# Message pass of a two-layer graph network: block sums added up in PSUM banks, one-hot matrices built on two engines, first LayerNorm inside the pass

## The reference

```python
# 6250 nodes, 256 features; 100000 edges (src, dst, edge_weight)
# layer 0: msg = (x[dst] @ node_w + node_b) * W(edge_weight)      W: radial basis and a small MLP
agg = segment_sum(msg, src)
h = x + agg
out = (h - mean(h)) / sqrt(var(h) + 1e-5) * ln_g + ln_b
x1 = layernorm(x + out * sigmoid(out @ gate_w + gate_b))
# layer 1: weighted means of x1's halves over the edges, both directions, added to x1, then a LayerNorm
```

## Time and profile before

| | us |
|---|---|
| median of 3 runs (lowest, highest) | 5071.47 (5069.38, 5073.18) |
| the profiled execution: its time | 5067.16 |
| its span, first to last instruction | 5065.1 |
| busy TensorE, VectorE, ScalarE, GpSimd | 3600.8, 2815.1, 2019.5, 3207.5 |

### The profile page before, as it was taken

How to read it: one execution, slowest core, us unless ns; L and a number is a source line. 1 busy time by engine, 2 the same in 40 slices (tenths; PEclk the granted TensorE clock), 3 DMA queues, 4 the chain that set the end, 5 groups by cost and what they waited for, 6 DMA issues and landing times.

```text
span 5065.1 us, 77985 instructions
## 1 busy us (share of the span) xinstructions
PE 3600.8 (71%) x16432; PEld 2653.5 (52%) x16433; DVE 2815.1 (56%) x7139; ACT 2019.5 (40%) x5492; POOL 3207.5 (63%) x3263
## 2 busy tenths in 40 slices
PE   6999999999999999788875544444443556565662
PEld 4655555555555555466653344444443555555552
DVE  4665656556566565466668522222222666666667
ACT  1555455554555545488884211111111222222221
POOL 0777777777777777600003477777777777777772
PEclk8999999999999999999997655555555776777775
DMA  7544444444444444476661111111111433334334
GB/s 191 134 136 135 135 138 136 137 135 135 137 135 136 135 135 138 137 226 216 215 212 40 32 53 53 53 53 53 53 53 59 113 102 102 102 105 107 102 102 77
DMA packets 464444, 588.32 MB, mean 116 GB/s; under 512 B 70163, under 2 KB 385171, under 8 KB 464406
## 3 DMA queue, kind: packets, MB, share of 16 engines
q0 software_dynamic: 128512, 317.64, 20.5%
q1 hardware_dynamic: 335894, 270.26, 18.9%
HBM read 391.39 MB, written 196.22 MB: 116 GB/s over the span
## 4 chain that ended last, share of the span: by engine, by line
POOL 41%; issue 23%; PE 12%; DVE 11%; DVEq 5%; DMA 4%; ACT 2%; POOLq 1%; SPq 0%; ACTq 0%
POOL s_rows L495 14%; POOL d_rows L528 14%; POOL arena L487 12%; DVE arena L1369 5%; DMA arena<-s_rows 3%; DVEq L313 3%; PE ps L908 3%; PE ps L989 3%; PE ps L980 2%; DVE agg L1234 1%; PE ps L933 1%; DVEq L1369 1%; DVE arena L1318 1%; ACT arena L643 1%; POOLq L287 1%
## 5 line engine op out<-in xcount | busy, mean ns | idle before, releaser
L528 POOL DMA_INDIRECT d_rows<-arena,adr x832 | 809.7, 973 | 302.8 <-issue 253.1
L487 POOL DMA_INDIRECT arena<-y_rows,idx x784 | 754.5, 962 | 354.2 <-issue 238.6
L541 POOL DMA_INDIRECT arena<-x_half,idx x832 | 808.2, 971 | 253.5 <-issue 250.2
L495 POOL DMA_INDIRECT s_rows<-arena,adr x784 | 770.4, 983 | 245.7 <-issue 244.8
L869 PE MATMUL ps<-f3s,arena 128*128 128x256 f32 x3136 | 728.2, 386 | 129.1 <-ACT arena L587 129.0
L958 PE MATMUL ps<-agg,arena 128*128 x1664 | 430.0, 440 | 521.7 <-ACT arena L699 521.6
L858 PE MATMUL ps<-arena,f2s 128*128 128x512 f32 x1568 | 706.1, 593 | 0.0
L869 PEld LDWEIGHTS ps<-f3s,arena 128*128 128x128 f32 x3136 | 581.1, 190 | 233.8 <-issue 120.9
L958 PEld LDWEIGHTS ps<-agg,arena 128*128 128x128 f32 x1664 | 370.0, 328 | 575.6 <-issue 575.6
L1369 DVE TENSOR_TENSOR arena<-arena,ps 128x129 f32 x1664 | 481.0, 289 | 333.0 <-issue 87.4
L989 PE MATMUL ps<-arena 128*128 128x129 f32 x1664 | 338.2, 367 | 425.4 <-issue 261.9
(11 more groups left out here) (195 smaller groups left out, 5850.9 us busy)
## 6 DMA issues: line engine op xcount, KB each, us to landing
arena<-s_rows SPq DMA_DIRECT2D x52, 2088.0 KB, 8.4
arena<-d_rows SPq DMA_DIRECT2D x52, 1040.0 KB
arena<-wrow SPq DMA_DIRECT2D x392, 64.0 KB
arena<-env_row SPq DMA_DIRECT2D x392, 64.0 KB
d_rows<-arena,adr POOLq DMA_INDIRECT x832, 2.3
arena<-x_half,idx POOLq DMA_INDIRECT x832, 2.5
s_rows<-tpl_s SPq DMA_DIRECT2D x98, 130.5 KB, 7.0
arena<-y_rows,idx POOLq DMA_INDIRECT x784
```

The lines of the kernel that those rows point to most:

```text
L487: pool.indirect_dma_start(gath[b][:, t, :], None, y_rows, bass.IndirectOffsetOnAxis(ap=idx[b][:, t:t + 1], axis=0)).then_inc(gathered[b], 16)
L495: pool.indirect_dma_start(s_rows, bass.IndirectOffsetOnAxis(ap=adr[b][:, t:t + 1], axis=0), msg[b][:, t, :], None).then_inc(scattered[b], 16)
L528: pool.indirect_dma_start(d_rows, bass.IndirectOffsetOnAxis(ap=adr[b][:, t:t + 1], axis=0), drow[b][:, t, :], None).then_inc(scattered_d[b ...
L541: pool.indirect_dma_start(gath2[b][:, t, :], None, x1_half, bass.IndirectOffsetOnAxis(ap=idx[b][:, t:t + 1], axis=0)).then_inc(gathered2[b ...
```

## The change

- In the pass every tile's product is accumulated by TensorE itself into one of four PSUM banks (SLOTS), the block's number modulo 4, at an offset that TensorE reads into a register from a new table slot_of; it reads the block number of the group's last tile too, and waits on a semaphore against it until that bank is free. VectorE no longer adds per tile: per block it waits for the block's last tile, adds the bank to x (`take_out`), and clears the bank.
- One-hots: ScalarE builds two tiles of four as before (BY_ACT = 2), GpSimd the other two with one is_equal each. The one-hot buffers are four instead of two, the message buffers four of 8 tiles (PT) instead of two of 16.
- x is loaded into agg during the message stage, block by block; the clearing of agg goes.
- The first LayerNorm is done by VectorE inside the pass, after each 7 blocks, with ln_g and ln_b (two operations of 128x1792). The roots come from a bit shift and three Newton steps on VectorE, twelve operations on 128x7.
- In the node stage that is left, transposes of chunk c + 1 are ahead of chunk c's gate products, with two buffers for each.
- Before the message stage: slot_of takes five operations on one partition, block ends two more, and each of two earlier computations loses two.

```diff
--- before.py
+++ after.py
...
+        s_buf = [take(PT, RW) for _ in range(4)]
+        hot = [take(GT, P) for _ in range(4)]
+        apart = [take(GT, P) for _ in range(2)]
         node_at = at
-        x_c = [take(CB * H) for _ in range(3)]
-        h_c = [take(CB * H) for _ in range(3)]
+        resid = take(NB * H)
+        h_c = [resid[:, c * CB * H:(c + 1) * CB * H] for c in range(CHUNKS)]
         at = 0
-        tr_c, gate_c, res_c = take(CB * H), take(CB * H), take(CB * H)
+        tr_c, gate_c = [take(CB * H) for _ in range(2)], [take(CB * H) for _ in range(2)]
...
+
+            for b in range(2):
+                sp.wait_ge(y_out[b], 16 * slot_uses(CHUNKS, b))
+            sp.wait_ge(table_mm, 2)
+            sp.dma_start(agg_n[:, 0:2, :], x_n[:, 0:2, :]).then_inc(x_in, 16)
             with sp.Fori(2, G0 // 4) as i:
                 for b in range(4):
                     load_de(4 * i + b, i, b)
                 blank_rest(i)
+                sp.dma_start(agg_n[:, bass.ds(i, 1), :], x_n[:, bass.ds(i, 1), :]).then_inc(x_in, 16)
 
             for b in range(4):
...
             def load_messages(c, q, b):
-                if not (fixed(c) and c < 2):
-                    hold(sp, agg_mm, 8 * c - 8)
-                    sp.wait_ge(rec_kept, c - 1)
-                sp.dma_start(s_buf[b], s_v[:, bass.ds(c * CT, CT), :]).then_inc(s_in[b], 16)
+                if not (fixed(c) and c < 4):
+                    hold(sp, agg_mm, PT * c - 3 * PT + 1)
+                    sp.wait_ge(rec_kept, c - 3)
+                sp.dma_start(s_buf[b], s_v[:, bass.ds(c * PT, PT), :]).then_inc(s_in[b], 16)
...
 
-            for c in range(CHUNKS):
-                h = by_block(h_c[c % 3])
-                pool.wait_ge(affine, c + 1)
-                G.tensor_tensor(h, h, gb[:, 0:1, :].to_broadcast([P, CB, H]), ALU.mult).then_inc(gained, 1)
-                pool.wait_ge(gained, c + 1)
-                G.tensor_tensor(h, h, gb[:, 1:2, :].to_broadcast([P, CB, H]), ALU.add).then_inc(normed, 1)
+
+            def one_hot(g, q, b):
+                c2, j = b // 2, b % 2
+                if j == 0:
+                    hold(pool, s_in[c2], 16 * q + 16)
+                if not (fixed(g) and g < 4):
+                    hold(pool, agg_mm, GT * g - 3 * GT + 1)
+                for t in range(BY_ACT, GT):
+                    last = G.tensor_scalar(hot[b % 4][:, t, :], lane[:, :], s_buf[c2][:, j * GT + t, H:H + 1],
+                                           None, ALU.is_equal)
+                last.then_inc(hotp_done, 1)
+
+            loop(pool, one_hot, G1, 8, 8, 0)
...
 
 
             def one_hot(g, q, b):
-                c2, j = b // 4, b % 4
+                c2, j = b // 2, b % 2
                 if j == 0:
                     act.wait_ge(s_in[c2], 16 * q + 16)
-                    A(rec[:, bass.ds(g * GT, CT), :], s_buf[c2][:, :, H:H + RF], ACT.Copy).then_inc(rec_kept, 1)
-                if not (fixed(g) and g == 0):
-                    act.wait_ge(hots_done, g)
-                for t in range(GT):
-                    last = A(apart[:, t, :], lane[:, :], ACT.Square, scale=-1.0,
+                    A(rec[:, bass.ds(g * GT, PT), :], s_buf[c2][:, :, H:H + RF], ACT.Copy).then_inc(rec_kept, 1)
+                if not (fixed(g) and g < 2):
+                    act.wait_ge(hots_done, g - 1)
+                for t in range(BY_ACT):
+                    last = A(apart[b % 2][:, t, :], lane[:, :], ACT.Square, scale=-1.0,
                              bias=s_buf[c2][:, j * GT + t, H:H + 1])
                 last.then_inc(apart_set, 1)
                 act.wait_ge(apart_set, g + 1)
-                if not (fixed(g) and g < 2):
-                    act.wait_ge(agg_mm, 2 * g - 2)
-                A(hot[b % 2], apart, ACT.Relu, scale=-1.0, bias=ones[:, 0:1]).then_inc(hots_done, 1)
+                if not (fixed(g) and g < 4):
+                    act.wait_ge(agg_mm, GT * g - 3 * GT + 1)
+                A(hot[b % 4][:, 0:BY_ACT, :], apart[b % 2][:, 0:BY_ACT, :], ACT.Relu, scale=-1.0,
+                  bias=ones[:, 0:1]).then_inc(hots_done, 1)
 
             loop(act, one_hot, G1, 8, 8, 0)
 
-            def std1_step(c):
-                act.wait_ge(var1_set, c + 1)
-                A(std1[:, :], var_eps1[:, :], ACT.Sqrt).then_inc(std1_set, 1)
-
             def transposes_out(c):
...
-                transposes_out(c)
-                if c + 2 < CHUNKS:
-                    std1_step(c + 2)
+                if c + 1 < CHUNKS:
+                    transposes_out(c + 1)
                 gates_out(c)
-                if c + 2 < CHUNKS:
-                    normalise1(c + 2)
-                std2_step(c)
 
             def turned_out(g, b):
...
             pe.wait_ge(msg_done, 2 * G0)
             pe.wait_ge(prod_done, 2 * G0)
+            for k in range(SLOTS):
+                last = mm(ps[:, 4 + k, 0:H], ident[:, :], f2s[:, 0, :], start=True, stop=False, skip_group_check=True)
+            last.then_inc(banks_open, 1)
+            slots = ps[:, 4:4 + SLOTS, :].rearrange("p a b -> p (a b)")
 
             def aggregate(g, q, b):
+                at = nc.values_load_multi_w_load_instructions(
+                    slot_of[0:1, bass.ds(g * GT, GT)], [mybir.EngineType.PE], min_val=0, max_val=(SLOTS - 1) * 512,
+                    skip_runtime_bounds_check_because="a number's last two bits, times 512")[1]
+
+                block_no = pe.value_load(slot_of[32:33, bass.ds(g * GT + GT - 1, 1)], min_val=1, max_val=NB)
+                pe.wait_ge(slot_free, block_no)
                 pe.wait_ge(hots_done, g + 1)
-                if not (fixed(g) and g < 4):
-                    pe.wait_ge(added, GT * g - 3 * GT)
+                pe.wait_ge(hotp_done, g + 1)
                 for t in range(GT):
-                    last = mm(ps[:, 2 * (b % 4) + t // 2, (t % 2) * H:(t % 2 + 1) * H], hot[b % 2][:, t, :],
-                              s_buf[b // 4][:, (b % 4) * GT + t, 0:H], start=True, stop=True)
-                    if t % 2:
-                        last.then_inc(agg_mm, 1)
-
+                    mm(slots[:, bass.ds(at[t], H)], hot[b % 4][:, t, :],
+                       s_buf[b // 2][:, (b % 2) * GT + t, 0:H], start=False, stop=False,
+                       skip_group_check=True).then_inc(agg_mm, 1)
+
+            pe.sem_inc(agg_mm)
             loop(pe, aggregate, G1, 8, 8, 0)
-            pe.wait_ge(added, GT * G1)
-
...
+            def turn_node(c):
                 pe.wait_ge(normed, c + 1)
...
+            turn_node(0)
+            pe.wait_ge(slot_free, SLOTS + NB)
             for c in range(CHUNKS):
-                node_products(c)
+                if c + 1 < CHUNKS:
+                    turn_node(c + 1)
+                gate_node(c)
...
+                        for p, off in ((32, 0.0), (0, -1.0)):
+                            last = V.tensor_scalar(slot_of[p:p + 1, k * (ST // 2):(k + 1) * (ST // 2)],
+                                                   ps[p:p + 1, 5 + k, 0:ST // 2], off, None, ALU.add)
+                    step(last)
+                    last = V.tensor_scalar(slot_of[0:1, :], slot_of[0:1, :], SLOTS - 1, 9,
+                                           ALU.bitwise_and, ALU.logical_shift_left)
                 last.then_inc(table_set, 1)
 
             def one_hot_rank(g, b):
...
-            V.memset(agg[:, :], 0.0).then_inc(agg_zero, 1)
-            dve.wait_ge(agg_zero, 1)
-
-            def add_up(g, q, b):
-                places = places_of(mybir.EngineType.DVE, 0, g, H)
-                for t in range(GT):
-                    if not (fixed(g) and g == 0 and t == 0):
-                        dve.wait_ge(added, GT * g + t)
-                    dve.wait_ge(agg_mm, 2 * g + t // 2 + 1)
-                    rows_of = agg[:, bass.ds(places[t], H)]
-                    V.tensor_tensor(rows_of, rows_of, ps[:, 2 * (b % 4) + t // 2, (t % 2) * H:(t % 2 + 1) * H],
-                                    ALU.add).then_inc(added, 1)
-
...
+
+            def inverse_root(of):
+
+                step(V.tensor_scalar(var_eps[:, :], of[:, :, 1], EPS_LN, None, ALU.add))
+                step(V.tensor_scalar(halved[:, :], var_eps[:, :].bitcast(i32), 1, None, ALU.logical_shift_right))
+                step(V.tensor_scalar(rstd[:, :].bitcast(i32), halved[:, :], -1.0, float(RSQRT), ALU.mult, ALU.add))
+                for _ in range(3):
+                    step(V.tensor_tensor(newton[:, :], rstd[:, :], rstd[:, :], ALU.mult))
+                    step(V.scalar_tensor_tensor(newton[:, :], newton[:, :], -0.5, var_eps[:, :], ALU.mult, ALU.mult))
+                    step(V.scalar_tensor_tensor(rstd[:, :], newton[:, :], 1.5, rstd[:, :], ALU.add, ALU.mult))
+
+            def normalise(to, src):
                 for j in range(CB):
-                    last = V.bn_stats(stats[:, j, :], by_block(src)[:, j, :])
+                    last = V.tensor_scalar(by_block(to)[:, j, :], by_block(src)[:, j, :], mv[:, j, 0:1],
```

(52 more changed lines are left out.)

163 lines of the change are left out of this document (42 added, 121 removed).

## The result

The changed kernel takes 5042.31 us (median of 5 runs, 5040.12 to 5046.69), the kernel before beside it 5071.47 (5 runs, 5067.46 to 5075.33): ratio 0.9947, 95% interval 0.9936 to 0.9959. Forecast were 4890 us and a range of 4845 to 4985. The kernel is faster by 29 us (0.5%), where 181 us (3.6%) were forecast. The profiled execution's span is 5038.4 us.

The account below looks back on a forecast made before the run. It took VectorE's chained additions to bound the pass, with TensorE and ScalarE close behind, and a ring through four engines the node stage. Terms -4 - 110.5 - 67 = -181.5 us took 5071.5 to 4890, range 4845 to 4985.

Parts of the forecast that it names:

- the sum: Whole kernel: -4 for the pass's head, -110.5 for the pass, -67 for the node stage, nothing elsewhere: -181.5 us.
- Head of the pass: Start of the pass: the halved first load lands after some 5.5 us and ScalarE's first one-hots halve: -4 us.
- The pass, 416 us with bounds 374 to 458: The pass: 208 groups at 2.0 us (1.8 to 2.2) make 416 us against 526.5: -110.5 us.
- The period of a group becomes the longest of these: The pass: the slowest of TensorE's array, its sequencer, ScalarE, GpSimd and loads sets a group's time, taken as 2.0 us.
- TensorE's sequencer, forecast at 1.9 us: The pass: two register loads, four tiles and some four waits or counters take 1.9 us a group, allowed 1.7 to 2.4.
- The rival of 2.4 us: The pass: TensorE's sequencer bounds it at 2.4 us a group, 83 us more, 4973; chance 0.17.
- the one of loads at 210 GB/s: The pass: loads hold it at 210 GB/s, 529 us, 113 more, 5003; chance 0.05.
- the rival on the other side: The pass: GpSimd's one-hots bound it at 3.06 us a group, 220 more, 5110, slower than before; chance 0.05.
- The clash of GpSimd and VectorE: The pass: the two disturb each other, costing VectorE 9 us and GpSimd some 6 of 60; the sum stays.
- The cover: The pass: VectorE's new work, about 20 us per 7 blocks, is hidden with 13 us to spare; uncovered, up to 12 a chunk.
- The node stage, 109: The node stage: 12 us before the gates, 91 for them and 6 to stage 4, against 175.9: -67 us.
- the cold-clock rival: The node stage: TensorE's clock stays low, 20 us a chunk, 49 more, 4939; chance 0.12.

Follow-up runs that it names:

- 13 writes: The changed kernel with 13 one-element memsets ahead of VectorE's part of the pass: 4881.12 us, ratio 0.9637 to the kernel before.
- 253 instructions: The changed kernel, its segment-sum loop on VectorE waiting once for two tiles, 32 of 285 instructions fewer: 6240.36 us, ratio 0.9669, on a slower chip.
- the one moved by 128: The changed kernel with 128 memsets ahead of VectorE's part of the pass: 5040.82 us, ratio 0.9951 to the kernel before.
- plain gathers: The changed kernel with stage 5's indirect gathers replaced by plain transfers of fixed rows, here with 28 memsets ahead of the pass: 5999.00 us, ratio 0.9218.

## Why the prediction was wrong

The step that failed is "From the first instruction of stage 4 on nothing changes, so the sum is made of what comes before it". The code doesn't change, and stage 4's time doesn't; but stage 5's loop stands in another place of VectorE's instruction stream, and stage 5 takes 153 us more, a term that the sum put at nothing. The cause is shown by runs: 13 instructions whose results nothing uses bring stage 5 to 1065 us, and the shift that the change makes, put alone into the kernel before, brings the stall about there (146 packets, stage 5 longer by 46 us on a slower chip). With 13 writes the kernel takes 4881.12 us, 184.6 less than the kernel before beside it; the sum said 181.5. That the sum comes so near is in part luck: the pass is 4 us longer than forecast and the node stage 8 shorter, and the node stage's sum has an error (below).

The other steps:

- Head of the pass, -4: -4.1. First use 5.3 us after the issue, against 5.5 until landing.
- The pass, 416 us with bounds 374 to 458: 419.6. "The period of a group becomes the longest of these" held. TensorE's sequencer, forecast at 1.9 us, is the longest with 1.97 from group to group, and with half the register reads a group takes 1.76, near the 1.72 of the array. The rival of 2.4 us fell, as did the one of loads at 210 GB/s: they moved 261, and 299 when asked.
- ScalarE 1.2 a group: 249.93 / 208 = 1.20. GpSimd's operation, 0.45 with ends at 0.31 and 1.28: busy 264.63 / 413 = 0.64. It had 1.3 of 1.97 us, so the rival on the other side stayed far.
- The clash of GpSimd and VectorE, 9 us for VectorE and 6 of 60 for GpSimd: GpSimd's busy time in the pass falls by some 21 us of 419, 3 of 60, when the LayerNorms go, and the pass by none. The cover was there. VectorE's 9 us weren't measured.
- The node stage, 109: 101.2. It is 12.4 us to the first gate, 82.9 for seven gates and 5.9 to stage 4. The sum's own figures don't add up here: seven gates of 12.4 are 87, and with "13 us for waits between them" 100, not 91, so the stage would have been 118. The 13 us were the mis-sized term: the gates follow one another 11.8 to 11.9 apart, without waits. TensorE's clock is 0.88 in the window against 0.72 in the earlier trace rows, and its sets take 1.13 us, so the cold-clock rival fell. Taking out the cover, LayerNorm behind the pass, costs 71 us.
- Elsewhere, nothing: the first load of the pass is issued 1.4 us later, stage 4 is 0.9 and the end 4.1 longer.

No rival had this mechanism. The profile before could have hinted at it: its instruction queue moved 24 packets while VectorE ran 19.7 thousand instructions, so loops ran without being fetched anew. That there is a limit, and that a loop of 285 was near it, nothing in that profile told.

## What to carry to other kernels

An edit that adds or removes instructions moves every later loop on that engine, and a long loop can begin to be fetched anew in each turn. After each change compare the packets of the instruction queue, and the waits "issue" that come once in a turn, before believing or blaming the edit; here a gain of 185 us looked like 29. Keep loop bodies short (here 253 instructions ran without the stall in the place where 285 had it), by waits that serve several instructions, and read registers for several groups at once where a sequencer has a gap.

## What the runs showed of the hardware

- VectorE's instructions come in pieces of 128: 1.20 MB in 147 packets is 8.2 KB each, five a turn in the bad places (147 packets against 27 with 13 writes, 120 in 24 turns), and the stalls lie 128 instructions apart. In the changed kernel's turn that begins with the branch at 4057.23, the five start 1.6 us before the branch and 3.3, 5.9, 8.3 and 29.3 after it; the next instruction starts at 5.3, and the first ones of the next three pieces at 7.7, 26.4 and 44.6. So each step into a piece seems to ask for the piece behind it, and the branch throws away what was asked for last. By this reading a loop that touches three pieces asks for four at most, one that touches four for five, and four find room; that is argued, not tested. It doesn't tell why 0.36 and 0.35 us are lost at pieces that were asked for 18 and 15 us ahead.
- The Trainium skill (Advanced Engine Details and Errata, section "ISA Cache") gives two lines of 256, of which the unmoved loop and the one moved by 128 can't both touch three. Both stall (147 and 148 packets), so for this kernel the measurement of 128 decides.
- The same kernel takes 5066 us on one chip and 6448 to 6507 on four others. The changed kernel's pass and node stage are as long on all, 419 to 420 and 101 us; the stages that scatter and gather single rows are the slower ones (stage 5 with its loop in a good place 1065 against 1347 to 1370 us, but 1050 on a slower chip with plain gathers). Why those chips are slower no run shows. A stall that costs stage 5 153 us on the first costs it 46 to 67 on the others, so what a mend is worth has to be measured on the chip that it is for.
